# Second pair of PSUM banks for two batches, scores in 32x32 tiles, and the narrow band masked by GpSimd, in a one-core convolution and attention block

## The reference

```
for ws in (9, 17):
    masked = where(|i - j| <= ws // 2, scores, -max)
    out = out + softmax(masked) @ v
out = out / 2
```

## Time and profile before

| | |
|---|---|
| device time, median of 3 | 101.0 us (100.86 to 103.18) |
| the profiled execution | 100.8 us, of which the span of the trace is 99.0 |
| granted clock of PE | 1.00 over the whole span |
| PE busy | 91.1 us of 99.0 |
| PE weight loads | 69.8 |
| DVE busy | 77.3 |
| ACT busy | 64.3 |
| POOL busy | 57.1 |
| a batch's input, issue to landing | 3.2 us (median of 8) |

### The profile page before, as it was taken

One profiled execution on the slowest core, in us unless ns is written; L12 is line 12 of the kernel. 1 busy time (PEld: TensorE's weight loads), 2 busy tenths in 40 slices (PEclk: granted clock), 3 DMA queues, 4 the chain that ended last, 5 costly groups with the idle time before them and its releaser, 6 DMA issues.

```text
span 99.0 us, 4555 instructions
## 1 busy us (share of the span) xinstructions
PE 91.1 (92%) x1909; PEld 69.8 (71%) x1909; DVE 77.3 (78%) x291; ACT 64.3 (65%) x178; POOL 57.1 (58%) x120
## 2 busy tenths in 40 slices
PE   4999489899999999999999999999999997989990
PEld 3678275794967986976888866978968765666660
DVE  1001625879998799999999999999999899966641
ACT  0535546759677665869865886898678658355450
POOL 5820204321796990858999078592957989940500
PEclk9999999999999999999999999999999999999999
DMA  0644500000000000000001001001001001010110
GB/s 18 180 94 155 190 0 0 7 0 0 10 0 7 7 7 0 7 0 0 7 0 58 1 7 36 27 0 53 6 7 56 3 7 56 0 58 2 57 28 28
DMA packets 4116, 2.91 MB, mean 29 GB/s; under 512 B 960, under 2 KB 4096, under 8 KB 4096
## 3 DMA queue, kind: packets, MB, share of 16 engines
q1 hardware_dynamic: 3872, 2.56, 8.4%
q10 hardware_dynamic: 224, 0.07, 0.3%
HBM read 1.57 MB, written 1.05 MB: 27 GB/s over the span
## 4 chain that ended last, share of the span: by engine, by line
PE 45%; DVE 32%; ACT 9%; issue 8%; POOL 2%; DVEq 0%; POOLq 0%
PE bank L335 10%; PE bank L246 7%; ACT q_four L600 5%; DVE prob_t L872 3%; DVE z_sb L842 3%; PE bank L315 3%; PE bank L358 3%; PE bank L292 2%; DVE v_win L849 2%; PE bank L326 2%; PE bank L319 2%; DVE st L894 2%; DVE t_sb L888 2%; DVE row_max L853 2%; PE bank L373 2%
## 5 line engine op out<-in xcount | busy, mean ns | idle before, releaser
L335 PE MATMUL bank<-k_pad,q_four 64*64 64x64 f32 x512 | 17.1, 220 | 0.2
L335 PEld LDWEIGHTS bank<-k_pad,q_four 64*64 64x64 f32 x512 | 15.7, 135 | 1.8 <-ACT q_four L600 0.9
L1177 POOL TENSOR_TENSOR rstd<-ve,minus_half 128x2 f32<-128x2 f32 x8 | 5.6, 703 | 18.9 <-DVE ve L836 18.9
L246 PE MATMUL bank<-warm_rows 128*128 128x256 bf16 x81 | 13.4, 299 | 1.2 <-DVE warm_rows L770 1.2
L600 ACT ACTIVATE q_four<-bank,four_mask 128x256 f32<-128x256 f32 x32 | 12.6, 484 | 0.0
L350 PEld LDWEIGHTS bank<-prob_t,v_win 32*32 32x32 f32 x1024 | 9.9, 104 | 3.4 <-issue 2.1
L1204 POOL TENSOR_TENSOR prob<-expd,row_inv 128x256 f32<-128x256 f32 x16 | 9.9, 617 | 3.5 <-DVE row_inv L868 3.5
L1198 POOL TENSOR_TENSOR diff<-narrow,row_max 128x192 f32<-128x192 f32 x16 | 8.2, 516 | 6.2 <-DVE row_max L853 6.1
L350 PE MATMUL bank<-prob_t,v_win 32*32 32x32 f32 x1024 | 11.1, 194 | 0.6 <-DVE prob_t L872 0.5
L853 DVE TENSOR_REDUCE row_max<-bank 128x16 f32<-128x512 f32 x16 | 10.6, 666 | 0.8 <-ACT narrow L607 0.8
L612 ACT ACTIVATE expd<-diff 128x448 f32<-128x448 f32 x16 | 9.2, 576 | 2.4 <-POOL diff L1198 1.5
(11 more groups left out here) (117 smaller groups left out, 212.5 us busy)
## 6 DMA issues: line engine op xcount, KB each, us to landing
x_all<-in_x_dram SPq DMA_DIRECT2D x8, 128.0 KB, 3.2
out_dram<-out_all SPq DMA_DIRECT2D x7, 128.0 KB, 2.5
qkv_rows<-in_L_attn_qkv_w_dram SPq DMA_DIRECT2D x1, 192.0 KB, 2.9
out_dram<-out_all SPq DMA_DIRECT2D x2, 64.0 KB, 1.5
proj_rows<-in_L_attn_proj_w_dram SPq DMA_DIRECT2D x1, 64.0 KB, 2.6
ffn_k<-in_L_ffn_kernel_dram SPq DMA_DIRECT2D x1, 64.0 KB, 2.2
proj_bias<-in_L_attn_proj_b_dram SPq DMA_DIRECT2D x1, 64.0 KB, 3.7
theta_w<-in_L_conv_w_theta_dram SPq DMA_DIRECT2D x1, 32.0 KB, 2.0
```

Source lines behind the costliest of these rows:

```text
L246: mm(bank[at][:, 0:TOK], warm_rows[:, 0:C], warm_rows[:, :], start=True, stop=True)
L335: last = mm(ps_scores[g][q, w, :, :], q_four[q, u % SLOTS, g * WB + w, :, :].rearrange("p e q -> p (e q)"), k_pad[q, u % SLOTS, at:at + KW ...
```

## The change

- Batches 1 and 3 do their first layer in banks 6 and 7 (`GUEST`); those banks are used by `weigh_values` and `turn_t2` only later, and these two get a wait for it at batch 0. `apply_bilinear(u)` and `project_g(u)` wait for the last batch before them in the same banks.
- `copy_kq` writes the queries twice, not four times, with every second head zeroed. `scores` uses four matmuls per window on tiles of 32x32, two heads in a tile, and streams the 32 keys once.
- `lay_mask` writes the wide mask alone, 256 columns. `copy_narrow` copies the 24 keys of the narrow band, not yet masked by it. A new POOL step `mask_narrow` adds the narrow mask, which `spread_narrow` (PE) and `keep_narrow_mask` (ACT) make once. `band_max` reduces the wide band alone, and a new DVE step `narrow_max` reduces the narrow one; `subtract_narrow` waits for it.
- The four lists of calls are written anew. `keep_warm` is called for 82 matmuls, before for 81.

```diff
+GUEST = (1, 3,)
-FOUR = 4
+EACH = 2
-SIDE = C // 2
+SIDE = C // PAIRS
+        def first_bank(u):
+            return bank[6] if u in GUEST else bank[0]
+        def second_bank(u):
+            return bank[7] if u in GUEST else bank[1]
+        def batches_before(u):
+            same = [p for p in range(u) if (p in GUEST) == (u in GUEST)]
+            return same[-1] + 1 if same else 0
...
+            def spread_narrow():
+                pe.wait_ge(masks_made, 1)
+                pe.wait_ge(weight_done, 3)
+                mm(bank[4][:, C:C + NW], query_sel[...], narrow_rows[:, :], start=True, stop=True)
...
             def apply_bilinear(u):
-                wait(pe, e_done, u)
-                mm(ps_u, bilinear_t[:, :], x_all[:, u, :], start=True, stop=True).then_inc(u_mm, 1)
+                wait(pe, e_done, batches_before(u))
+                mm(first_bank(u)[:, 0:TOK], bilinear_t[:, :], x_all[:, u, :], start=True, stop=True).then_inc(u_mm, 1)
...
             def project_g(u):
-                wait(pe, z_done, u)
+                wait(pe, z_done, batches_before(u))
...
             def lay_mask(u, g):
-                mm(bank[4 + g][:, :], query_sel[...], key_mask[:, g:g + WB, :, :]..., start=True, stop=False)
+                mm(bank[4 + g][:, 0:WB * KW], query_sel[...], key_mask[:, g:g + WB, :]..., start=True, stop=False)
             def scores(u, g):
                 for w in range(WB):
-                    for i in range(2):
+                    for i in range(PAIRS):
                         q = slice(SIDE * i, SIDE * (i + 1))
-                        last = mm(ps_scores[g][q, w, :, :], q_four[q, u % SLOTS, g * WB + w, :, :]...,
-                                  k_pad[q, u % SLOTS, at:at + KW].unsqueeze(1).to_broadcast([SIDE, KINDS, KW]), ...)
+                        last = mm(ps_scores[g][q, w, :], q_pair[q, u % SLOTS, g * WB + w, :, :]...,
+                                  k_pad[q, u % SLOTS, at:at + KW], ...)
             def weigh_values(u, g):
+                if u == 0 and g == 0:
+                    pe.wait_ge(e_done, GUEST[-1] + 1)
             def turn_t2(u, s=None):
+                if u == 0:
+                    pe.wait_ge(z_done, GUEST[-1] + 1)
...
             def copy_narrow(u, g):
-                nc.scalar.copy(narrow[:, u % SLOTS, g], ps_scores[g][:, :, 1, INSET:INSET + NW])
+                nc.scalar.copy(near[:, u % SLOTS, g], ps_scores[g][:, :, INSET:INSET + NW])
...
             def band_max(u, g):
-                v.tensor_reduce(row_max[:, u % SLOTS, g], ps_scores[g], AX.X, ALU.max).then_inc(max_done[g], 1)
+                v.tensor_reduce(row_max[:, u % SLOTS, g, 0], ps_scores[g], AX.X, ALU.max).then_inc(max_done[g], 1)
+            def narrow_max(u, g):
+                dve.wait_ge(narrow_made[g], u + 1)
+                v.tensor_reduce(row_max[:, u % SLOTS, g, 1], narrow[:, u % SLOTS, g], AX.X, ALU.max).then_inc(nmax_made[g], 1)
...
+            def mask_narrow(u, g):
+                pool.wait_ge(narrow_kept[g], u + 1)
+                p.tensor_tensor(narrow[:, u % SLOTS, g], near[:, u % SLOTS, g],
+                                narrow_mask[:, :].unsqueeze(1).to_broadcast([C, WB, NW]), ALU.add).then_inc(narrow_made[g], 1)
             def subtract_narrow(u, g):
-                pool.wait_ge(max_done[g], u + 1)
+                pool.wait_ge(nmax_made[g], u + 1)
```

More of the change, by code:

```diff
@@ L971, in _ @@
+            turn_probs(1, 0)
             pick_odd(0)
[L972 removed]
             window_values(2)
[L974 to L975 removed]
             residual(0)
[L977 to L978 removed]
+            row_sums(2, 1)
+            subtract_max(2, 0)
+            narrow_max(2, 0)
+            norm_first(4)
+            turn_probs(1, 1)
+            row_inverse(2, 1)
             stats_second(0)
[L980 to L981 removed]
```

693 lines of the change are left out of this document (365 added, 328 removed).

## The result

| | before, same chip | after |
|---|---|---|
| device time, median | 101.1 us (4 runs) | 103.28 us (103.11 to 104.49, 4 runs) |
| profiled execution, its span | 100.8, 99.0 | 103.11, 101.4 |

The ratio is 1.0249 (95% interval 1.0149 to 1.0349): slower, though not shown to be slower by the 2% that the prediction reckoned with. The forecast was 99.2 us and the range ended at 101.0: the miss is 4.1 us and outside the range.

A forecast was written before the change was run, and what follows sets the result against it. DVE was taken to bound the long stretch from 35.58 us on. The span: 99.0 - 2.4 (start) + 0.3 (maxima) + 0.5 (POOL's path) - 0.2 (end) = 97.2, plus 2.0 = 99.2 us; range 97.2 to 101.0.

The forecast's parts named there:

- the one on scores: PE's score matmuls: 128 at 9.7 ns per two calls, 0.77 us less per batch, 6.2 us of PE in all.
- The start: Up to `residual(0)`: batch 1 no longer waits for batch 0's banks; gain 2.4 us, lower end 1.0.
- The walk: Stepping through the new lists with old instruction slots to time the start; it leaves out small hand-overs.
- First band maximum to `residual(0)`: Second stage: DVE's only gap 0.45 us, `residual(0)` at 34.9 instead of 35.58, with 1.7 us of later work done.
- The middle: From `residual(0)` to `turn_probs(7, 1)`: POOL's longer path adds 0.5 us of DVE idle, making 1.4.
- the values named for the rivals: DVE idle from `residual(0)` to `turn_probs(7, 1)`: under 0.8 us for one rival, 3 and more, mostly POOL's, for two others.
- The end: After `turn_probs(7, 1)`: earlier `pick_odd(7, 1)` and `norm_second(7, 1)` gain 0.2 us, between 0 and 0.5.
- The maxima: DVE's band reductions, split into wide and narrow: 0.3 us more work over sixteen groups, bounds 0.2 to 1.0.
- POOL becomes the chain: DVE's `narrow_max` waits for POOL's `mask_narrow`, 0.85 us per exposed group; 103 to 106 us, chance 0.07.
- The scores cost their old price per instruction: Each new score matmul on PE takes 31 ns, 16 us more of PE; about 112 us, chance 0.01.
- The reading of the rule there: Skill's about 60 cycles per matmul: 9.7 ns was taken to speak against it for tiles working side by side.
- The clock: Named as making the forecast wrong: a granted PE clock under the 1.00 that all stages had.

The follow-up runs named there:

- m_dense: Kernel after plus 2048 matmuls 32x32 and 1024 of 64x64, results unread, behind PE's last instruction; one execution, in which the 2048 took 56 us.
- b_pair: Kernel before with two heads to a 32x32 tile and nothing else, both bands still streamed and masked by PE; 111.0 us, ratio 1.0898 to before.
- a_early: Kernel after with the transfer of input 2 issued right behind proj_rows, nothing else; 101.4 us, no ratio made.
- a_early_fewer: Kernel after with input 2 issued early and half of weigh_values' windows in batches 0 to 6 replaced by warm matmuls; 99.75 us, ratio 0.985 to before.
- a_fewer: Kernel after with half of weigh_values' windows in batches 0 to 6 replaced by three warm matmuls of equal time; 100.53 us, ratio 0.9985 to before.
- b_once: Kernel before, old banks and lists, 64x64 tiles, with keys streamed once and the narrow band masked by POOL; 111.5 us, ratio 1.1009 to before.
- b_guest: Kernel before with the second pair of banks for batches 1 and 3 and nothing else; 102.35 us, no ratio.
- b_shift: Kernel before with its first 12 warm matmuls of 256 columns cut into 48 of 64, the same expected time; 102.32 us, ratio 1.0182 to before.
- a_early_half: Kernel after with input 2 issued early and scores in bf16, one pass instead of two, 512 matmuls fewer; 101.97 us.

## Why the prediction was wrong

**The step that failed** is the one on scores. It priced PE by busy time ("128 instructions per two calls, so 1.24 us, and 0.77 us less per batch"), booked this as time that PE gives back, and put the supply of instructions at nothing. The price was right: 128 took 1.31 us at 30.98, as in `weigh_values` in the earlier trace rows. But those matmuls are also 512 more, and in a dense run a block of 128 takes 3.45 to 4 us to come (m_dense). Before, 64x64 tiles at 31 ns used a block up in about that time. After, two calls use one up in 1.2 us, and PE stands if the next isn't there. With the tiles alone changed this costs 7.8 us of holes (b_pair). The number was in the rows that the prediction rests on: x64 beside x128 in the earlier trace rows. It was costed as time only.

In spans, 97.2 us was forecast and 101.4 measured. Of these 4.2 us, 0.8 came in the start, 2.7 up to `residual(0)` and 0.7 behind it; the holes are about 2.1 of the 2.7. Without them the changed kernel is about as fast as the one before: m_dense is at `turn_probs(7, 1)` at 88.51, and with after's 11.1 us behind it that would be a span of 99.6 (an estimate), against 99.0 before and 101.4 in after. So the holes explain most of why the change is slower, and half of the miss; the forecast gain wasn't there without them either. By the terms of the sum:

- *The start.* `norm_first(0)` 13.0 was forecast and came at 13.62, `norm_first(1)` 15.5 at 16.13, `norm_first(2)` 20.0 at 20.78, the first band maximum 20.65 at 21.43. The walk let `mix_tokens(0)` end at 11.1, and it ended at 11.63, behind the 1.32 us for input 2. By the first band maximum that is 0.8 us. Such times also depend on when the clock of PE rises: a_early and a_early_fewer have the same start list, and `fold_bilinear` took 0.48 us in one and 0.79 in the other, at 3.92 us in both; the first `norm_first` came at 12.03 and 13.05.
- *First band maximum to `residual(0)`.* 14.25 us forecast (20.65 to 34.9), 16.95 measured, 14.8 in the kernels without a hole in the scores. The holes are 2.1 us; the 0.6 that is left was not taken apart.
- *The middle.* Idle 1.4 forecast, 2.14 measured. It lies between the values named for the rivals; by the waits it isn't POOL's alone, and a_fewer has 1.99 there, without a hole, so this part is not holes.
- *The end.* 0.2 forecast; idle 5.97 became 5.87. In size, nothing.
- *The maxima.* DVE's work rose by 0.6 us instead of 0.3, within the bounds given.

**The rivals.** "POOL becomes the chain" holds the measured time (103.3 in 103 to 106), but not by its mechanism: the wait that it named is not in the table of after, the second stage without holes is 14.73 us without the mask and 14.81 with it, and a_fewer has the time of before with POOL's work unchanged. With the old lists (b_once) that wait is there, 6.1 us. "The scores cost their old price per instruction" had the right object, the instruction, and the wrong price: what counts is not 31 ns each, it is 3.5 to 4 us per 128. The reading of the rule there, that 9.7 ns speak against a fixed cost per matmul, was right for the pace of a run and said nothing on how long a run can be kept up: the 128 of the earlier trace rows are one block.

**The clock.** The prediction said that a clock under 1.00 would make it wrong. It fell in after behind a stretch in which PE worked 13.60 us of 16.95 (two slices of the page, 5 and 8 tenths). 64 matmuls of `weigh_values` took 1.07 us there, where 64 took 0.75 at 42.77, and a pair that takes 0.70 took 1.22:

```profile
38.86 1.07 PE L372 MATMUL bank<-prob_t,v_win 32*32 32x32 f32 x64
39.87 1.22 PE L335 MATMUL bank<-zt_sb,qkv_t 128*128 128x256 f32 x2
```

That is 1.2 GHz for about 3.4 us, and at most 1.7 us of PE work lost in it. It lies behind the holes of the second stage, so it isn't what opened them; and a_fewer and m_dense have one such fall too and are 1.8 to 2.0 us ahead of after at `turn_probs(7, 1)`.

## What to carry to other kernels

Count a tuned engine's instructions, not only their time: take the number in a block (here 128 matmuls with their weight loads), see how fast the list uses one up, and compare with the distance between two blocks in a dense run. On PE here a sustained pace of over 128 matmuls in 3.5 to 4 us can't be fed, and a list near that pace has no slack for a block that comes late, so splitting a matmul into smaller tiles can leave PE's busy time the same or lower and the kernel slower. And a saving on an engine that is not the bound is worth nothing, while what it costs elsewhere is paid.

When an edit removes a cost, check that the cost stood behind the edit in time. a_fewer gave 2.7 us back by its medians, and the two large holes that it lost lay over 6 us ahead of the first instruction that it left out.

## What the runs showed of the hardware that was not expected

- One packet of 16 KB holds 256 instructions; PE's dense small matmuls get one every 3.45 to 4.0 us (m_dense, nearly all of it at a granted clock of 0.50). In m_dense and after they go on 2.3 to 2.7 us after it has moved.
- A hole's place follows the count of instructions (217 matmuls and a multiple of 127 more), whether it opens does not: the same 2423 matmuls had five holes in after, two in a_early and none in m_dense. Its size varies (0.2 to 2.3 us), and it can stand ahead of a large matmul. A kernel with 1909 matmuls can have one too, when its steps move (b_guest 1.79 us, b_shift 0.99).
- A float32 matmul on a 64x64 tile costs 31 ns with 64 columns and with 32; on 32x32 tiles, four side by side, 9.7 ns with 32.
- With less to do, PE loses its clock: 0.92 to 0.97 in the four executions with 1911 matmuls (a_early_half, no hole in its trace), 1.00 in all four of a_early_fewer, with 2017 matmuls and PE 1.6 us busier.
